# The attention-out projection and router norm of 24 row tiles in the last unit of the first attention

## The chip, the cores and the metric

One core of a Trainium2 chip runs the whole program. The metric is the device time in microseconds (us); the median of three runs is given, and one more execution was profiled. PE is TensorE (PEld its weight loads), DVE VectorE, ACT ScalarE, POOL GpSimd, SP SyncE.

## The reference

Four layers run one after the other on x of 4 x 1024 x 128, in float32, each on the layer norm of its input and added to it. The change touches the seam between the first two:

```
x = x + u + concat_heads(softmax(q k^T / sqrt(8)) v) @ w_out + b_out     # u = layernorm(x), 16 heads of 8; q, k, v from a second norm of u
z = layernorm(x)                                                     # (x - mean) * rsqrt(var + 1e-5)
logits = z @ Wr^T + rb                                               # 8 experts, the two best weighted by their sigmoid
x = x + shared(z) + sum over e of weight_e * expert_e(z)             # expert(z) = silu(z Wg^T) * (z Wu^T) @ Wd^T
```

After them come a differential attention and a feed-forward layer in blockwise FP4, which the change leaves as they are.

## The kernel before

The residual x lies in SBUF as 32 row tiles of 128 rows, which are 8 chunks of 4 tiles (two chunks to a batch element). The program is a row of blocks; each block gives every engine its own list of instructions, engines meet at a block's end, and within a block they are ordered by semaphores alone. There is no scheduler: the order in the code is the order on each engine.

**First attention** (`attention_phase`, from L419). It works in 16 units (a batch element and 4 heads of 8 channels). A unit has 16 steps k, eight for each half of the queries. In a step PE makes four score matmuls (L719; 51 rows of bf16 parts, 512 queries), ACT takes the exponential of each into `probs` (L656), and PE multiplies the probabilities of two steps earlier with v (L694). Scores go round three PSUM banks, so a score waits for the exponential three before it. The product with v stands after the second score of a step, in the steps k = 2 and 10 after the fourth. In these two steps ACT also copies a finished half of the output (L644, at the head of its step), PE transposes it back to rows (L702), and DVE divides it by the row sums into `o_units` (L601, L604). Beside this, PE and DVE compute the maxima of the next unit's scores (L676, L572). The last unit has no next one, so its banks 3 to 6 are nearly free, and DVE does little in it but round the FP4 weights (`fp4_round`, L622, with lines L2204 to L2250) in step k = 2. POOL is idle from the start of the attention, where it adds u and b_out to x.

**Weight transposes** (`transpose_jobs`, L946 to L964) are a block of their own.

**Router phase** (`attention_out_and_router_phase`, from L751), again a block. Each chunk goes through these stages, every engine taking several chunks at different stages in turn (`steps`, L776):
transposes of the attention output (PE L793), copy to SBUF (ACT L831), projection with w_out (PE L802, two passes to a matmul), addition to x (DVE L859), statistics (DVE L105, L109), 1/deviation and shift (POOL L116, L118, L883, L886), normalised rows z (ACT L840), transposes of z (PE L810), two copies of them, `zb` and the rounded `zH` (ACT L848, L849), the remainder `zL` (DVE L866), logits (PE L818) and their bias (DVE L871). A bank pair serves each of the four PSUM uses, so a chunk waits for the chunk two before it.

**Experts** (`experts_phase`, from L1102) begin with DVE's choice of experts, and SP loads the weights of the next attention.

Of the kernel before, what the change touches and what calls it, by code (L numbers as in the profile page):

```python
# [20 lines left out]
F32 = mybir.dt.float32  # L21
# [6 lines left out]
P = 128  # L28
# [118 lines left out]
class Stacks:  # L147
# [7 lines left out]
    def __init__(self, core, ctx, q_parts_dram, k_parts_dram):  # L155
# [6 lines left out]
        self.neg_rest, self.neg_parts = sb("neg_max_rest", [pairs, P]), sb("neg_max_parts", [pairs, PARTS, P], BF16)  # L162
        self.u, self.bo = sb("u", [P, core.tiles, core.C]), sb("b_out_rows", [P, core.C])
# [255 lines left out]
def attention_phase(core, v_units, o_units, stacks, fp4_weights, later):  # L419
# [55 lines left out]
    with ExitStack() as ctx:  # L475
# [20 lines left out]

        def units(engine, unit):


            for u in range(UNITS):  # L500
                unit(u, u // RING, u % RING, u % 2)
# [25 lines left out]
        with nc.Block() as block:  # L527
# [135 lines left out]
            def _(pe):  # L663
# [87 lines left out]
def attention_out_and_router_phase(core, o_units, w, zH, zL, logits, wrT, rb):  # L751
# [5 lines left out]
    nc, ps, C = core.nc, core.ps, core.C  # L757
    E = wrT.shape[1]
    TC = BANK // P
    CHUNKS = core.tiles // TC  # L760
    OT, OUT, ZT, LOGITS = 0, 2, 4, 6
    Z, TZ, LG = 2, 3, 4
    with ExitStack() as ctx:
        sb = lambda name, shape, dt=F32: sbuf(core.nc, ctx, name, shape, dt)
        oT, z, zb = sb("o_chunk_T", [P, 2, BANK]), sb("z_rows", [P, 2, TC, C]), sb("z_chunk_T", [P, 2, BANK])
        norm = Norm(core, ctx, "router", TC, CHUNKS)
        shift = sb("router_shift", [P, CHUNKS, TC])
        oT_psum, oT_ready = semaphore(core, "o_chunk_T_psum"), semaphore(core, "o_chunk_T_ready")
        out_psum, x_done = semaphore(core, "out_psum"), semaphore(core, "out_added")
        shifted, z_ready, zT_psum = semaphore(core, "router_shift_ready"), semaphore(core, "z_ready"), semaphore(core, "zT_psum")  # L770
        zb_ready, zH_done, zL_done = semaphore(core, "z_chunk_T_ready"), semaphore(core, "expert_zH_done"), semaphore(core, "expert_zL_done")
        lg_psum, lg_done = semaphore(core, "logits_psum"), semaphore(core, "logits_done")
        tile = lambda t: slice(t * P, (t + 1) * P)
        tiles = lambda c: slice(c * TC, (c + 1) * TC)

        def steps(*stages):  # L776

            for s in range(CHUNKS + LG):
                for lag, stage in stages:
                    if 0 <= s - lag < CHUNKS:  # L780
                        stage(s - lag)

        with nc.Block() as block:

            @block.tensor
            def _(pe):

                def transpose_o(c):
                    b, half = divmod(c, 2)
                    if c >= 2:  # L790
                        pe.wait_ge(oT_ready, c - 1)
                    for t in range(TC):
                        ins = nc.tensor.transpose(ps[:, OT + c % 2, tile(t)],  # L793
                                                  o_units[:, half * TC + t, b * GROUP:(b + 1) * GROUP, :].rearrange("p g c -> p (g c)"), core.ident[:])
                    ins.then_inc(oT_psum, 1)

                def project_o(c):
                    pe.wait_ge(oT_ready, c + 1)
                    if c >= 2:
                        pe.wait_ge(x_done, c - 1)  # L800
                    for t in range(TC):
                        ins = nc.tensor.matmul(ps[:, OUT + c % 2, tile(t)], oT[:, c % 2, tile(t)], w[:], start=True, stop=True)  # L802
                    ins.then_inc(out_psum, 1)

                def transpose_z(c):
                    pe.wait_ge(z_ready, c + 1)
                    if c >= 2:
                        pe.wait_ge(zL_done, c - 1)
                    for t in range(TC):
                        ins = nc.tensor.transpose(ps[:, ZT + c % 2, tile(t)], z[:, c % 2, t, :], core.ident[:])  # L810
                    ins.then_inc(zT_psum, 1)

                def make_logits(c):
                    pe.wait_ge(zb_ready, c + 1)
                    if c >= 2:
                        pe.wait_ge(lg_done, c - 1)
                    for t in range(TC):
                        ins = nc.tensor.matmul(ps[:, LOGITS + c % 2, t * E:(t + 1) * E], zb[:, c % 2, tile(t)], wrT[:],  # L818
                                               start=True, stop=True)
                    ins.then_inc(lg_psum, 1)  # L820

                steps((0, transpose_o), (TZ, transpose_z), (LG, make_logits), (0, project_o))

            @block.scalar
            def _(act):

                def copy_oT(c):
                    act.wait_ge(oT_psum, c + 1)
                    if c >= 2:
                        act.wait_ge(out_psum, c - 1)  # L830
                    nc.scalar.copy(oT[:, c % 2, :], ps[:, OT + c % 2, :]).then_inc(oT_ready, 1)  # L831

                def make_z(c):
                    act.wait_ge(norm.inverse, c + 1)
                    act.wait_ge(shifted, 2 * c + 2)
                    if c >= 2:
                        act.wait_ge(zT_psum, c - 1)
                    for t in range(TC):
                        n = c * TC + t
                        ins = nc.scalar.activation(z[:, c % 2, t, :], core.x[:, n, :], ACT.Identity,  # L840
                                                   bias=shift[:, c, t:t + 1], scale=norm.rstd[:, n:n + 1])
                    ins.then_inc(z_ready, 1)

                def take_zT(c):
                    act.wait_ge(zT_psum, c + 1)
                    if c >= 2:
# [1621 lines left out]
```

## Time and profile before

| | us |
|---|---|
| median of 3 runs | 2914.62 (2912.93 to 2914.83) |
| the profiled execution | 2917.84 |
| its span, first to last instruction | 2916.1 |
| PE busy in the span | 2753.1 (94%) |
| DVE busy | 2377.3 (82%) |
| ACT busy | 1997.7 (69%) |
| POOL busy | 1040.0 (36%) |
| mean granted TensorE clock | 0.975 of full |

The 3.2 us between the median and the profiled execution are to be kept in mind when stretches of the profile are subtracted from the median. A granted clock of 1.00 is 2.4 GHz and one of 0.50 is 1.2 GHz. Busy PE time contains the latency of matmuls, so a busy PE can still have room. The last unit of the attention runs from about 748 to 792 us, the weight transposes to 801, the router phase to 843.

### The profile page before, as it was taken

Reading aid. Unit: us, or ns where it says so; the run is one execution under the profiler, and the core shown is the slowest. Engines: PE = TensorE matmul, PEld = TensorE weight load, DVE = VectorE, ACT = ScalarE, POOL = GpSimd, SP = SyncE. Lnnn points to the kernel's source line nnn. Section 1 sums busy time; section 2 is a strip of 40 time slices with the busy share of each in tenths; the row PEclk is TensorE's granted clock in tenths of the full one; section 3 lists DMA queues with packets and bytes.
Section 4 is the critical chain, followed back from the end, with each engine's and each line's share of the span. In section 5 each row is a group of like instructions: output and inputs, shape, how many; then the busy total and the mean of one; then the engine's idle time right before and its main releaser. Section 6 shows DMA issues by size and latency. Waiting matters only on the chain.

```text
span 2916.1 us, 43834 instructions
## 1 busy us (share of the span) xinstructions
PE 2753.1 (94%) x14770; PEld 1820.7 (62%) x14770; DVE 2377.3 (82%) x3982; ACT 1997.7 (69%) x3999; POOL 1040.0 (36%) x1558
## 2 busy tenths in 40 slices
PE   4799999999889999899999999999999999999996
PEld 2122222222278888777777777777777777777774
DVE  6999999999355555677777888888888889888887
ACT  5288888888742232477777777777777777777773
POOL 4200000000010000145555665555555556555561
PEclk8699999999979999999999999999999999999998
DMA  2220000000010000000000000000000000000000
GB/s 66 87 80 19 17 23 23 17 18 13 1 59 1 1 1 1 1 1 1 1 1 1 1 1 1 1 1 1 8 1 1 1 1 8 1 1 1 1 1 15
DMA packets 31023, 34.98 MB, mean 12 GB/s; under 512 B 7656, under 2 KB 18896, under 8 KB 30672
## 3 DMA queue, kind: packets, MB, share of 16 engines
q1 hardware_dynamic: 30800, 32.18, 3.7%
q8 instruction: 119, 1.95, 0.3%
q14 instruction: 104, 0.85, 0.1%
HBM read 23.37 MB, written 8.39 MB: 11 GB/s over the span
## 4 chain that ended last, share of the span: by engine, by line
PE 49%; DVE 8%; issue 2%; ACT 0%; POOL 0%; POOLq 0%; DVEq 0%; ACTq 0%
PE ps L1613 7%; PE ps L1614 7%; PE ps L1618 7%; PE ps L1552 7%; PE ps L1540 7%; DVE neg_maxima L1821 3%; PE ps L1568 2%; PE ps L1570 1%; PE ps L1569 1%; PE ps L1558 1%; PE ps L1557 1%; PE ps L1556 1%; PE ps L1529 1%; PE ps L1530 1%; PE ps L1531 1%
## 5 line engine op out<-in xcount | busy, mean ns | idle before, releaser
L1821 DVE TENSOR_REDUCE neg_maxima<-ps 128x1 f32<-128x1024 f32 x512 | 624.7, 1220 | 147.9 <-PE ps L1618 144.9
L656 ACT ACTIVATE probs<-ps 128x512 f32<-128x512 f32 x1024 | 535.1, 606 | 172.4 <-PE ps L719 172.2
L1763 ACT ACTIVATE diff_probs<-ps,neg_maxima 128x1024 f32<-128x1024 f32 x512 | 575.6, 1124 | 92.4 <-DVE neg_maxima L1821 90.4
L572 DVE TENSOR_REDUCE maxima_of_halves<-ps 128x2 f32<-128x1024 f32 x512 | 602.4, 1220 | 17.3 <-PE ps L676 12.8
L1613 PE MATMUL ps<-z_T_high,y_high 128*128 128x512 f32 x1024 | 464.9, 454 | 5.6 <-ACT diff_probs L1763 5.6
L2095 POOL TENSOR_TENSOR DT_low<-DT_whole,DT_high 128x512 fp32r<-128x512 f32 x256 | 334.9, 1308 | 351.8 <-DVEq L1989 306.4
L1614 PE MATMUL ps<-z_T_low,y_high 128*128 128x512 f32 x1024 | 404.5, 395 | 0.0
L1833 DVE SCALAR_TENSOR_TENSOR D<-diff_probs,ratio 128x1024 f32<-128x1024 f32 x256 | 330.1, 1290 | 9.4 <-DVE ratio L1829 0.4
L719 PE MATMUL ps<-q_stacks,k_stacks 51*128 51x512 bf16 x1024 | 314.1, 386 | 20.6 <-ACT probs L656 14.7
L1618 PE MATMUL ps<-z_T_high,y_low 128*128 128x512 f32 x1024 | 319.5, 393 | 0.0
L1540 PE MATMUL ps<-identity,D 128*128 128x128 f32 x2048 | 307.6, 273 | 1.7 <-ACT arena L1705 1.7
L676 PE MATMUL ps<-k_stacks,q_stacks 48*128 48x512 bf16 x1024 | 253.8, 403 | 40.9 <-DVE maxima_of_halves L572 32.6
L1540 PEld LDWEIGHTS ps<-identity,D 128*128 128x128 f32 x2048 | 254.5, 140 | 51.5 <-ACT arena L1705 2.6
L694 PE MATMUL ps<-probs,v_and_one 128*32 128x512 f32 x2048 | 274.9, 609 | 0.2 <-ACT probs L656 0.2
L719 PEld LDWEIGHTS ps<-q_stacks,k_stacks 51*128 51x128 bf16 x1024 | 77.4, 94 | 316.3 <-ACT probs L656 282.7
L116 POOL TENSOR_SCALAR router_rstd<-router_moments 128x4 f32<-128x4 f32 x8 | 1.8, 228 | 730.4 <-DVE router_moments L109 730.4
L1202 ACT ACTIVATE silu_gate<-ps 128x512 f32<-128x512 f32 x144 | 85.9, 597 | 246.8 <-PE ps L1173 246.8
L1720 ACT ACTIVATE squares<-ps,inverse_sums 128x256 f32<-128x256 f32 x256 | 122.4, 478 | 158.7 <-PE ps L1570 151.7
L1552 PE MATMUL ps<-arena,z_tiles 128*128 128x512 f32 x512 | 230.5, 593 | 0.0
L1613 PEld LDWEIGHTS ps<-z_T_high,y_high 128*128 128x128 f32 x1024 | 193.6, 189 | 54.8 <-issue 16.1
L1614 PEld LDWEIGHTS ps<-z_T_low,y_high 128*128 128x128 f32 x1024 | 194.2, 190 | 46.1 <-issue 15.1
L1618 PEld LDWEIGHTS ps<-z_T_high,y_low 128*128 128x128 f32 x1024 | 193.1, 189 | 45.2
(301 smaller groups left out, 5009.8 us busy)
## 6 DMA issues: line engine op xcount, KB each, us to landing
q_stacks<-q_parts_dram SPq DMA_DIRECT2D x192, 32.0 KB
q_parts_dram<-qk_parts SPq DMA_DIRECT2D x12, 256.0 KB, 2.4
k_parts_dram<-qk_parts SPq DMA_DIRECT2D x12, 256.0 KB, 3.4
k_stacks<-k_parts_dram SPq DMA_DIRECT2D x32, 96.0 KB
residual<-in_L_attn_x_dram SPq DMA_DIRECT2D x4, 512.0 KB, 6.2
k_stacks<-k_parts_dram SPq DMA_DIRECT2D x32, 64.0 KB
q_stacks<-neg_max_parts SPq DMA_DIRECT2D x96, 4.0 KB, 1.7
out_dram<-residual SPq DMA_DIRECT2D x3, 512.0 KB, 3.2
```

The source lines that it names most:

```text
L572: nc.vector.tensor_reduce(mx_half[:, own, half, :, p * PB + t, :], ps[:, bank:bank + 2, :], X, ALU.max).then_inc(nat_max, 1)
L656: nc.scalar.activation(probs[:, k % PT, h, :], ps[:, (r + k + i) % S_RING, :], ACT.Exp, scale=SCALE).then_inc(s_free, 1)
L719: nc.tensor.matmul(ps[:, (r + k + i) % S_RING, :], kst[rows, r, p, kb * P:(kb + 1) * P], qst[rows, r, p, half * BANK:(half + 1) * BANK], s ...
L1540: ins = nc.tensor.transpose(ps[:, T_BANK, k * P:(k + 1) * P], D[:, t % 2, kb * P:(kb + 1) * P], core.ident[:])
L1552: nc.tensor.matmul(ps[:, UY, :], z[:, k, :], DT[:, g, k, :], start=k == 0, stop=False)
L1613: nc.tensor.matmul(ps[:, 2 * m + c, :], a, high[:, keys], start=True, stop=False)
L1614: nc.tensor.matmul(ps[:, 2 * m + c, :], a, low[:, keys], start=False, stop=False)
L1618: ins = nc.tensor.matmul(ps[:, 2 * m + c, :], a_low, high[:, keys], start=False, stop=True)
L1763: nc.scalar.activation(probs[:, t % 2, m, :], ps[:, 2 * m:2 * m + 2, :].rearrange("p k n -> p (k n)"), ACT.Exp, bias=neg[:, t, m:m + 1], a ...
L1821: nc.vector.tensor_reduce(neg[:, t, m:m + 1], ps[:, 2 * m:2 * m + 2, :].rearrange("p k n -> p (k n)"), X, ALU.max, negate=True).then_inc(m ...
L1833: nc.vector.scalar_tensor_tensor(D[:, t % 2, :], probs[:, t % 2, 1, :], ratio[:, t:t + 1], probs[:, t % 2, 0, :], ALU.mult, ALU.add).then_ ...
L2095: pool.tensor_tensor(DT_low[:, t // G, :, q], DT_whole, DT_high[:, t // G, :, q].bitcast(F32), ALU.subtract).then_inc(DT_split, 1)
```

## The change

- Chunks 0 to 5 (24 row tiles) are transposed (even steps 0 to 10) and projected (odd steps 1 to 11) inside the last attention unit, at the end of the step on PE, in banks 4 and 6. DVE, not ACT, copies the transposes to SBUF there, then adds to x and takes the statistics. `fp4_round` comes after the last of these chunks.
- POOL computes 1/deviation of these chunks in the same block, and the normalised rows of chunks 0 to 3. Rows of chunks 4 and 6 are ACT's, of 5 and 7 DVE's.
- The router phase projects only chunks 6 and 7 and does the rest of the stages for all eight. The order on each engine is written out.
- z rows get six slots, in the place of `u`. `gate` and `h` of the experts are allocated earlier.

```diff
@@ attention_phase: GpSimd
                 pool.tensor_tensor(core.x[:], core.x[:], stacks.bo[:].rearrange("p (o c) -> p o c", o=1).to_broadcast(
-                    [P, core.tiles, core.C]), ALU.add)
+                    [P, core.tiles, core.C]), ALU.add).then_inc(u_added, 1)
+                pool.wait_ge(u_added, 2)
+                for c in range(router.FRONT):
+                    router.deviation(pool, c)
+                    if c < router.POOL_ROWS:
+                        router.pool_rows(pool, c)
@@ attention_phase: VectorE
-                        if k == LAG and not exists(u + 1):
-                            dve.wait_ge(fp4_weights.arrived, 16 * len(fp4_weights.loads))
-                            fp4_round(dve, fp4_rounder, stepper(dve, fp4_rounded), fp4_weights.w[:], fp4_weights.w[:])
                         if k == PB + LAG:
                             divide_o(u, 0, *turn_of(u, odd, ("o", 0)))
+                        if k in chunk_out and not exists(u + 1):
+                            c = chunk_out[k]
+                            if c == 0:
+                                dve.wait_ge(u_added, 2)
+                            router.wait_oT(dve, c)
+                            nc.vector.tensor_copy(router.oT[:, c % 2, :], ps[:, CHUNK_OT, :]).then_inc(router.oT_ready, 1)
+                            router.add(dve, c, CHUNK_OUT)
+                            if c == router.FRONT - 1:
+                                dve.wait_ge(fp4_weights.arrived, 16 * len(fp4_weights.loads))
+                                fp4_round(dve, fp4_rounder, stepper(dve, fp4_rounded), fp4_weights.w[:], fp4_weights.w[:])
@@ attention_phase: TensorE, at the end of a step
+                        if k in chunk_T and not exists(u + 1):
+                            if k == 0:
+                                pe.wait_ge(nat_max, last_turn + 1 + NAT0)
+                                pe.wait_ge(expert_weights.arrived, 16 * len(expert_weights.loads))
+                            router.transpose_o(pe, chunk_T[k], o_units, CHUNK_OT, chunk_T[k] > 0)
+                        if k in chunk_out and not exists(u + 1):
+                            router.project_o(pe, chunk_out[k], expert_weights.w_out, CHUNK_OUT, chunk_out[k] > 0)
@@ class Router (the stages of the old function, with these new or different)
+    SLOTS = 6
+    FRONT = 6
+    POOL_ROWS = 4
+    ACT_ROWS, DVE_ROWS = (4, 6), (5, 7)
...
+    def deviation(self, pool, c):
+        norm, shift = self.norm, self.shift[:, c, :]
+        norm_rstd(norm, pool, c, c)
+        if c in self.ACT_ROWS:
+            use = 2 * self.ACT_ROWS.index(c)
+            pool.wait_ge(norm.inverse, c + 1)
+            pool.tensor_tensor(shift, norm.moments[:, self.tiles(c), 0], norm.rstd[:, self.tiles(c)], ALU.mult).then_inc(self.shifted, 1)
+            pool.wait_ge(self.shifted, use + 1)
+            pool.tensor_scalar(shift, shift, -1.0, None, ALU.mult).then_inc(self.shifted, 1)
+
+    def pool_rows(self, pool, c):
+        pool.wait_ge(self.norm.inverse, c + 1)
+        for t in range(self.TC):
+            ins = norm_rows(self.norm, pool, self.z[:, c, t, :], self.core.x[:, c * self.TC + t, :], c * self.TC + t)
+        ins.then_inc(self.z_pool, 1)
@@ router_phase
+                for c in last:
+                    router.transpose_o(pe, c, o_units, OT + c % 2, False)
+                router.transpose_z(pe, 0)
+                router.transpose_z(pe, 1)
+                for c in last:
+                    router.project_o(pe, c, w, OUT + c % 2, False)
+                for c in range(router.CHUNKS):
+                    router.make_logits(pe, c, zb, wrT)
+                    if c + 2 < router.CHUNKS:
+                        router.transpose_z(pe, c + 2)
...
+                for c in last:
+                    router.wait_oT(act, c)
+                    act.copy(router.oT[:, c % 2, :], core.ps[:, OT + c % 2, :]).then_inc(router.oT_ready, 1)
+                for c in range(router.CHUNKS):
+                    if c == 2:
+                        router.scalar_rows(act, 4)
+                    if c == 5:
+                        router.scalar_rows(act, 6)
+                    router.take_zT(act, c, zb, zH)
...
+                router.vector_rows(dve, 5)
+                for n, c in enumerate(last):
+                    router.add(dve, c, OUT + c % 2)
+                    router.low_z(dve, n, zH, zL)
+                router.take_logits(dve, 0, logits, rb)
+                for c in range(2, router.CHUNKS):
+                    if c == 3:
+                        router.vector_rows(dve, 7)
+                    router.low_z(dve, c, zH, zL)
+                    router.take_logits(dve, c - 1, logits, rb)
+                router.take_logits(dve, router.CHUNKS - 1, logits, rb)
...
+                for c in last:
+                    router.deviation(pool, c)
```

A norm row (`norm_rows`) is one tensor_scalar with two per-row operands, 128x128 in and out, on the engine that it is given.

## Rows read from the trace of the kernel before

**Rows 1.** Windows: us and instructions busy per engine, granted clock, DMA.
```profile
750.00:790.00 40.00, 32.61 (x198) 7.65 (x194) 10.31 (x14) 31.42 (x62) 0.00 (x0) 0.96 0.00 0
...
800.00:844.80 44.80, 35.29 (x195) 32.82 (x196) 23.85 (x104) 25.16 (x58) 13.66 (x32) 0.67 0.00 1
```

**Rows 2.** Timeline of one step of the last unit: start, duration, instruction.
```profile
762.68 2.06 ACT L656 ACTIVATE probs<-ps 128x512 f32<-128x512 f32 x4 [0.33 <-PE ps L719]
...
763.33 0.39 PE L719 MATMUL ps<-q_stacks,k_stacks 51*128 51x512 bf16 x1 [0.47 <-ACT probs L656]
763.65 1.06 PE L694 MATMUL ps<-probs,v_and_one 128*32 128x512 f32 x8
...
764.64 0.60 PE L719 MATMUL ps<-q_stacks,k_stacks 51*128 51x512 bf16 x3
765.07 2.06 ACT L656 ACTIVATE probs<-ps 128x512 f32<-128x512 f32 x4 [0.33 <-PE ps L719]
```

**Rows 3.** Timeline of the router phase, PE.
```profile
801.47 1.09 PE L793 MATMUL ps<-identity,arena 128*128 128x128 f32 x4 [1.69 <-PEq L934]
...
806.83 2.08 PE L802 MATMUL ps<-w_out,o_chunk_T 128*128 128x128 f32 x8 [0.68 <-ACT o_chunk_T L831]
...
815.93 0.60 PE L810 MATMUL ps<-identity,z_rows 128*128 128x128 f32 x4
...
816.36 0.96 PE L818 MATMUL ps<-wrT,z_chunk_T 128*128 128x8 f32 x8
...
817.18 1.14 PE L802 MATMUL ps<-w_out,o_chunk_T 128*128 128x128 f32 x8
...
818.15 0.60 PE L793 MATMUL ps<-identity,arena 128*128 128x128 f32 x4
```

**Rows 4.** Timeline of the last unit where ACT copies the output, k = 10.
```profile
773.21 0.59 ACT L644 COPY oT<-ps 128x512 f32<-128x512 f32 x1
...
776.74 1.08 ACT L656 ACTIVATE probs<-ps 128x512 f32<-128x512 f32 x2 [0.97 <-PE ps L719]
```

**Rows 5.** Windows and timeline where the granted clock is at its lower level.
```profile
754.00:756.00 2.00, 2.00 (x10) 0.82 (x6) 0.37 (x2) 0.14 (x1) 0.00 (x0) 0.50 0.00 0
...
810.00:814.00 4.00, 3.56 (x16) 3.38 (x16) 2.34 (x13) 2.52 (x7) 1.72 (x4) 0.50 0.00 0
...
756.19 1.08 ACT L656 ACTIVATE probs<-ps 128x512 f32<-128x512 f32 x2 [2.05 <-PE ps L719]
```

**Rows 6.** Timeline of the router phase, DVE and ACT.
```profile
805.34 0.69 DVE L859 TENSOR_TENSOR residual<-ps,residual 128x512 f32<-128x512 f32 x1 [4.20 <-PE ps L802]
...
807.11 0.38 DVE L109 BATCH_NORM_AGGREGATE router_moments<-router_stats 128x2 f32<-128x6 f32 x4
...
815.44 0.56 ACT L848 COPY z_chunk_T<-ps 128x512 f32<-128x512 f32 x1
...
816.52 0.69 DVE L866 TENSOR_TENSOR z_T_low<-ps,z_T_high 128x512 fp32r<-128x512 f32 x1 [1.53 <-ACT z_T_high L849]
...
817.18 1.65 ACT L840 ACTIVATE z_rows<-residual,router_shift,router_rstd 128x128 f32<-128x128 f32 x4 [0.21 <-issue]
```

**Rows 7.** Timeline, the end of the router phase.
```profile
842.85 0.19 DVE L871 TENSOR_TENSOR logits<-ps,rb_rows 128x32 f32<-128x32 f32 x1 [1.32 <-PE ps L818]
```

**Rows 8.** Timeline of DVE in the last unit: the FP4 rounding, the last divide.
```profile
756.10 1.34 DVE L2204 TENSOR_REDUCE fp_weights_scale<-fp_w 128x72 f32<-128x1152 f32 x1
...
764.35 1.36 DVE L2250 TENSOR_TENSOR fp_w<-fp_weights_scaled,fp_weights_scale 128x1152 f32<-128x1152 f32 x1
...
791.23 0.26 DVE L601 RECIPROCAL recip<-ps 128x16 f32<-128x16 f32 x1 [14.21 <-PE ps L702]
```

**Rows 9.** Groups by line, POOL: busy us, mean ns, idle before.
```profile
L2095 POOL TENSOR_TENSOR DT_low<-DT_whole,DT_high 128x512 fp32r<-128x512 f32 x256 | 334.9, 1308 | 351.8 <-DVEq L1989 306.4 <-ACT DT_high L1705 41.2 <-DVEq L2029 2.5
...
L118 POOL TENSOR_TENSOR router_rstd<-router_rstd,minus_half 128x4 f32<-128x4 f32 x8 | 8.3, 1036 | 0.7 <-POOL router_rstd L116 0.2
...
L1304 POOL CAST M_head<-M 128x256 fp32r<-128x256 f32 x32 | 12.5, 392 | 34.0 <-ACT M L1374 34.0
```

More of the change, by code:

```diff
@@ L495, in attention_phase @@
         S0, NAT0, PV0 = S_RING, NAT_BUFS, PT
+        CHUNK_OT, CHUNK_OUT = NAT + 1, NAT + 3
+        chunk_T = {2 * c: c for c in range(router.FRONT)}
+        chunk_out = {2 * c + 1: c for c in range(router.FRONT)}
+        last_turn = taken[UNITS - 2, ("shift", 0)]
         def units(engine, unit):
@@ L748, in _ @@
                 transpose_o(UNITS - 1, 1, *turn_of(UNITS, 0, ("o", 1)))
-def attention_out_and_router_phase(core, o_units, w, zH, zL, logits, wrT, rb):
-    nc, ps, C = core.nc, core.ps, core.C
-    E = wrT.shape[1]
+class Router:
     TC = BANK // P
-    CHUNKS = core.tiles // TC
-    OT, OUT, ZT, LOGITS = 0, 2, 4, 6
-    Z, TZ, LG = 2, 3, 4
-    with ExitStack() as ctx:
[L764 to L783, printed above, removed]
@@ new lines, in transpose_o, with project_o @@
+    def transpose_o(self, pe, c, o_units, bank, reused):
+        b, half = divmod(c, 2)
+        if reused:
+            pe.wait_ge(self.oT_ready, c)
+        for t in range(self.TC):
+            ins = pe.transpose(self.core.ps[:, bank, self.tile(t)],
+                               o_units[:, half * self.TC + t, b * GROUP:(b + 1) * GROUP, :].rearrange("p g c -> p (g c)"), self.core.ident[:])
+        ins.then_inc(self.oT_psum, 1)
+    def project_o(self, pe, c, w, bank, reused):
+        pe.wait_ge(self.oT_ready, c + 1)
+        if reused:
+            pe.wait_ge(self.x_done, c)
+        for t in range(self.TC):
+            ins = pe.matmul(self.core.ps[:, bank, self.tile(t)], self.oT[:, c % 2, self.tile(t)], w[:], start=True, stop=True)
+        ins.then_inc(self.out_psum, 1)
@@ new lines, in make_logits, with wait_oT @@
+    def make_logits(self, pe, c, zb, wrT):
+        E = wrT.shape[1]
+        pe.wait_ge(self.zb_ready, c + 1)
+        if c >= 2:
+            pe.wait_ge(self.lg_done, c - 1)
+        for t in range(self.TC):
+            ins = pe.matmul(self.core.ps[:, self.LOGITS + c % 2, t * E:(t + 1) * E], zb[:, c % 2, self.tile(t)], wrT[:],
+                            start=True, stop=True)
+        ins.then_inc(self.lg_psum, 1)
+    def wait_oT(self, engine, c):
+        engine.wait_ge(self.oT_psum, c + 1)
+        if c >= 2:
+            engine.wait_ge(self.out_psum, c - 1)
@@ new lines, in wait_slot, with scalar_rows @@
+    def wait_slot(self, engine, c):
+        engine.wait_ge(self.norm.inverse, c + 1)
+        if c >= self.SLOTS:
+            engine.wait_ge(self.zT_psum, c - self.SLOTS + 1)
+    def scalar_rows(self, act, c):
+        self.wait_slot(act, c)
+        act.wait_ge(self.shifted, 2 * self.ACT_ROWS.index(c) + 2)
+        for t in range(self.TC):
+            n = c * self.TC + t
+            ins = act.activation(self.z[:, c % self.SLOTS, t, :], self.core.x[:, n, :], ACT.Identity,
+                                 bias=self.shift[:, c, t:t + 1], scale=self.norm.rstd[:, n:n + 1])
+        ins.then_inc(self.z_act, 1)
@@ new lines, in pool_rows, with router_phase @@
+    def pool_rows(self, pool, c):
+        pool.wait_ge(self.norm.inverse, c + 1)
+        for t in range(self.TC):
+            ins = norm_rows(self.norm, pool, self.z[:, c, t, :], self.core.x[:, c * self.TC + t, :], c * self.TC + t)
+        ins.then_inc(self.z_pool, 1)
+def router_phase(core, router, o_units, w, zH, zL, logits, wrT, rb):
+    OT, OUT = 0, 2
+    with ExitStack() as ctx:
+        zb = sbuf(core.nc, ctx, "z_chunk_T", [P, 2, BANK])
+        last = range(router.FRONT, router.CHUNKS)
+        with core.nc.Block() as block:
@@ L797, in project_o @@
[L797 to L811, printed above, removed]
@@ L2431, in program @@
         fp4 = Fp4Transposed(core, ctx, fp4_weights)
+        router = Router(core)
+        with ExitStack() as ahead_of_rows:
+            router.place_norm(ahead_of_rows)
         rows = DifferentialRows(core, ctx)
```

146 lines of the change are left out of this document (72 added, 74 removed).

## The prediction

> **What bounds the kernel now.** I read the busy times by stretch first [rows 1]. In the last attention unit (750 to 790 us) PE is busy for 32.6 of 40 us and ACT for 31.4; nothing is saturated there. In the router phase (800 to 844.8) PE shows 35.3 of 44.8 us at a mean granted clock of 0.67, while DVE and ACT are busy for a little over half and POOL for 13.7: a chain that hands chunks from engine to engine, with TensorE often at its lower level. All engines meet at the end of each block, so a microsecond taken out of either stretch is a microsecond of the span, provided that nothing behind waits for it.
>
> Second, one regular step of the last unit in order of time [rows 2]. The exp at 762.68 frees a bank; the score matmul at 763.33 takes it (0.65 us later), the products with v start at 763.65 (0.32), the next scores at 764.64 (0.99), and their exp at 765.07 (0.43): 2.39 us. In this loop ACT works 2.06 and stands 0.33, and PE waits 0.47 before the score at 763.33. So there is a hole in PE, but the loop through PE and ACT is closed: what is put on PE is free only as far as it fits in the hole.
>
> Third, the pieces of the router phase [rows 3 to 6], and where it ends: the last logits at 842.85 + 0.19 = 843.04 [rows 7].
>
> **The change part by part.**
>
> *What the last unit takes on.* Per chunk of four row tiles PE gets four transposes T (in even steps 0 to 10) and four projections P (odd steps 1 to 11), all behind the step's last score. Prices at the full clock: T 0.43 us (815.93 to 816.36), P 0.97 (817.18 to 818.15); at the half clock T shows 1.09 and P 2.08, the latency of the last instruction with them [rows 3], so I take 0.87 and 1.8 from start to start.
> A P starts about 0.2 us before the loop's reference exp (its two scores start 0.43 ahead of that exp and take some 0.2 to 0.3), so it ends 0.8 after it. The next scores start there, not at once; the second of them was due at 0.65. The products with v then start at about 0.8 + 0.32 = 1.12 to 1.25 in place of 0.97: 0.15 to 0.3 us later, and I take 0.3 for steps 3, 5, 7 and 11 = 1.2. In steps 1 and 9 ACT copies oT next in any case (0.59 us in front of the exps) [rows 4], which covers a P: 0.05 each. A T ends 0.3 after the reference exp, before anything is due: 0.05 each for steps 0, 4, 6, 8. In steps 2 and 10 the unit's own transposes already let ACT run dry (0.97 us idle before the exp at 776.74 [rows 4]); a second T there costs itself, 0.5 with the change-over, twice = 1.0. Sum 1.2 + 0.1 + 0.2 + 1.0 = **+2.5 us**. Bounds: below, 0 (no piece can make the unit faster, except that a busier PE might spare the half-clock stretch of [rows 5], worth at most 1.1 us: the stall of 2.05 there against 0.97 in the same place of the other half); above, every piece in full, 6 x (0.97 + 0.43) = 8.4.
>
> *DVE in the last unit.* Copy, addition and statistics per chunk: 0.69 + 2.15 (805.34 to 807.49) [rows 6] = 2.8 us in 4.8 us of two steps. The copy has a whole step between T and P, so no wait enters PE. fp4_round (756.10 to 765.71, 9.6 us) [rows 8] moves from step 2 behind the last chunk. The last P starts near 778.0 in old time, ends at 779.0, its addition and statistics at 781.3, the rounding at 790.9; the last divide, which is queued behind it, was released at 791.23 [rows 8]. So the margin is 0.3 us, more by what the last P delays the rest. I put 0 for it; if DVE is late by a microsecond, that is on the path, for the block's end waits for this divide.
>
> *POOL.* Deviations of six chunks and rows of four. A deviation costs 1.04 for the power [rows 9], and I allow 0.8 for its small instructions. A row instruction (128x128, one tensor in) stands nowhere; from below a cast of 128x256 takes 0.39, from above a 128x512 with two tensors 1.31 [rows 9]; I take 0.5, for it is nearer to the cast. A chunk is then 1.8 + 4 x 0.5 = 3.8 us, at the upper bound 7.0; six chunks beginning at 753 end by 782, or by 785 at the upper bound, and the first reader (transpose of z chunk 0) stands at 803. Hidden at either end.
>
> *What the router phase gives.* Chunks 6 and 7 alone are still projected there; eight are transposed, split and given logits. It begins as before at 801.47 [rows 3], TensorE at the half clock until about 814 [rows 5]. PE's order: T6, T7, z0, z1, four pieces of 0.87: 804.9. P6, P7 at 1.8: 808.5. Logits 0 (a P's price, eight passes): 810.3. z2 wants the low part of chunk 0, which DVE makes behind addition and statistics of chunk 6: 807.0 + 2.15 + 0.69 = 809.9, in time. z2 811.2, logits 1 813.0, z3 813.9, logits 2 about 815.0. From here, at the full clock, PE needs 0.97 + 0.43 = 1.4 us a chunk and is no longer the bound; z4 ends 815.5, logits 3 816.5. DVE makes rows 7 in four instructions (1.3 us; below 0.69 by the price of 512 elements in the addition, above 1.65, ACT's [rows 6]) at 813.7 to 815.1, so low 3 ends at 815.8 and z5 at 817. ACT takes z4 (zb 0.56 [rows 6], and zH as long, overlapping: 1.0 together) until 816.7 and only then makes rows 6 (1.65), until 818.4: z6 waits for it and ends at 818.9. ACT's copies of chunk 5 end at 819.4, of 6 at 820.4; low 5 at 820.2, z7 820.7, zb 7 at 821.4, logits 7 822.6, the addition of rb 823.0. Against 843.04: **-20.0 us**. Bounds by the clock, with the same order: half speed to the end, 2.7 us a chunk on PE, ends at 828.9 (-14.1); full speed from the start, bound by DVE and ACT, ends at 818.9 (-24.1).
>
> *What stands behind.* SP's loads of the next attention's weights start at the next block and shift with it; its first waits are on instructions, not on clock time. gate and h only get other addresses. The PE wait for expert weights in step 0 is long met. All 0.
>
> Sum: 2.5 - 20.0 = -17.5. The profiled execution took 2917.84 us (span 2916.1); it would become 2900.3. The median of the three timed runs is 2914.62, 3.2 below the profiled one, and the forecast for the median is 2914.62 - 17.5 = **2897.1**.
>
> **The rivals.**
> - *The half clock holds through the router phase.* For it: it holds from 801 to 814 and returns several times later, mean 0.67 [rows 1, 5]. Against: PE will be idle less than before. -14.1 + 2.5 = -11.6: 2903.0.
> - *The full clock comes early*, since attention's end keeps PE busier: 2.5 - 24.1 = -21.6: 2893.0. For it, the same sentence; against, the start of this phase stays what it is, a block's end with PE idle 1.7 us [rows 3].
> - *The pieces cost their full price in the last unit*, because the loop of [rows 2] has less play than I drew: 8.4 - 20.0 = -11.6: 2903.0 too. For it: ACT is only 0.33 from being full. Against: PE's wait of 0.47 in each step.
> - *Slower: the last unit falls to the half clock.* Its place is the 38 us of the unit; the profile shows one such stretch in it, 754 to 757 [rows 5]. There the loop of [rows 2] would take 3.75 (the products with v doubled, the scores' latency up by a half), with a T or P in PE 4.3 on the mean, against 2.39 and 2.6: 12 x 1.7 + 4 x 1.4 = +26. Net -17.5 + 26 = +8.5: 2923. It makes the kernel slower only where over two thirds of the unit run so. Against it: 0.96 mean clock in the unit with less work on PE than it will have [rows 1].
> - *DVE late.* The rounding has 0.3 us to spare, and POOL's last deviation (1.8 us) runs beside its start. If DVE stood still for that time, the last divide would come 1.5 late: -16.0, 2898.6; with as much again in the last chunk's statistics, -14.2, 2900.4. For it: four of the rounding's ten instructions read two SBUF tensors. Against: POOL's power takes 1.04 us [rows 9] in the router phase while DVE works too [rows 6], with no sign of either being held up. The Trainium skill (GPSIMD Engine Reference, Key points) has the rule for it: GpSimd shares its SBUF interfaces with VectorE, and contends with DVE instructions that have two SBUF inputs or run in a 2-port mode. The rows cited have no such DVE instruction beside POOL, so they don't decide on that rule.
>
> **How the numbers follow.** Forecast 0.45; half clock 0.14, early full clock 0.17, full price 0.13, DVE late 0.07, slower 0.03; 0.01 for a gain undone elsewhere. 0.2% is 5.8 us, about what can be told from no change here. All but the last two lie beyond it unless half clock and full price meet (-5.7). So faster 0.92, same 0.05, slower 0.03. The range reaches from the early clock with a free unit (-23) to half clock with two thirds of the full price (-8): 2892 to 2907.
>
> **What would show it.** The last unit (first scores of unit 15 to the last divide) should be 2 to 4 us longer, its steps 3, 5, 7 and 11 at 2.6 to 2.7 us and its plain even ones at 2.4. The first weight transpose should follow the last divide by 0.6 us as before, and the divide should wait for PE. POOL's rows should last 0.4 to 0.8 each. The router phase should be 21 to 23 us from its first transpose to the last logits, half clock until about 814. From the expert phase on every stretch should keep its length. The forecast is wrong if steps with a P take over 3 us, if DVE's rounding ends after the last transposes, or if z transposes wait for rows.

## The result and the profile after

The changed kernel takes 2896.2 us (median of four runs, 2894.97 to 2896.72) against 2913.77 of the kernel before (four runs): 17.6 us less, ratio 0.9939 (0.9922 to 0.9956). The forecast was 2897.1. The profiled execution took 2894.97 us, its span is 2893.1.

I cut both profiles by instructions that exist in both: VectorE's copy of v for the last unit, the last divide, the last logits, the first and the last maximum of the second attention. Instructions by line in the kernel before: durations in ns (min/median/max), then the first and the last start in us.

```profile
L608 DVE COPY v_and_one<-arena x16: 271/284/285, 119.3 to 740.5; 128x256 f32<-128x256 f32 x16
L601 DVE RECIPROCAL recip<-ps x32: 257/257/258, 148.3 to 791.2; 128x16 f32<-128x16 f32 x32
L1821 DVE TENSOR_REDUCE neg_maxima<-ps x512: 1210/1219/1226, 1210.9 to 2842.8; 128x1 f32<-128x1024 f32 x171
```
The same in the changed kernel, and its logits:
```profile
L622 DVE COPY v_and_one<-arena x16: 273/283/284, 118.0 to 738.6; 128x256 f32<-128x256 f32 x16
L615 DVE RECIPROCAL recip<-ps x32: 257/258/259, 146.4 to 790.1; 128x16 f32<-128x16 f32 x32
L911 DVE TENSOR_TENSOR logits<-ps,rb_rows x8: 179/180/193, 808.4 to 822.4; 128x32 f32<-128x32 f32 x8
L1920 DVE TENSOR_REDUCE neg_maxima<-ps x512: 1209/1219/1227, 1189.6 to 2819.1; 128x1 f32<-128x1024 f32 x171
```

| stretch | before | after | difference |
|---|---|---|---|
| start to the v copy of the last unit | 740.5 | 738.6 | -1.9 |
| v copy to the last divide ("the unit") | 50.7 | 51.5 | +0.8 |
| last divide to the last logits ("the phase") | 51.6 | 32.4 | -19.3 |
| last logits to the first maximum | 368.1 | 367.2 | -0.9 |
| first to last maximum of the second attention | 1631.9 | 1629.5 | -2.4 |
| the rest of the span | 73.3 | 74.0 | +0.7 |

Differences are taken from hundredths (the last divide is at 791.23 and 790.06, the last logits at 842.85 [rows 7] and 822.42). "The phase" contains the weight transposes, which take the same time in both; the router phase itself, from its first transposes to the last logits, went from 41.4 us (801.47 to 842.85) to 22.1 (800.30 to 822.42).

The change made the second and third rows, -18.5 together. The rest of the profiles' difference of 22.9 is of the size of the scatter of single executions: it lies in stretches with the same instructions, and the v copy of the other kernels' profiles below lies between 738.6 and 740.9.

The last unit after, timeline, steps with a P (L833) and a T (L824) between two full exp rows of ScalarE:
```profile
757.60 2.06 ACT L677 ACTIVATE probs<-ps 128x512 f32<-128x512 f32 x4 [0.17 <-PE ps L740]
...
759.57 0.39 PE L740 MATMUL ps<-q_stacks,k_stacks 51*128 51x512 bf16 x2
759.89 1.16 PE L833 MATMUL ps<-w_out,o_chunk_T 128*128 128x128 f32 x8
759.99 1.08 ACT L677 ACTIVATE probs<-ps 128x512 f32<-128x512 f32 x2 [0.33 <-PE ps L740]
...
760.98 0.39 PE L740 MATMUL ps<-q_stacks,k_stacks 51*128 51x512 bf16 x2
...
761.46 1.08 ACT L677 ACTIVATE probs<-ps 128x512 f32<-128x512 f32 x2 [0.38 <-PE ps L740]
...
762.62 0.66 PE L824 MATMUL ps<-identity,arena 128*128 128x128 f32 x4
762.72 2.06 ACT L677 ACTIVATE probs<-ps 128x512 f32<-128x512 f32 x4 [0.17 <-PE ps L740]
```
Two steps take 5.12 us (757.60 to 762.72) where two of before take 4.78 (twice the 2.39 of [rows 2]): 0.34 us for a P and a T together, which add 1.40 us of work to PE.

The half clock near step 2 of the kernel before cost more than the one stall of [rows 5]. ScalarE before, in steps 2 and 3 and in the same place of the other half, steps 10 and 11:
```profile
752.04 2.10 ACT L656 ACTIVATE probs<-ps 128x512 f32<-128x512 f32 x4
...
757.90 2.06 ACT L656 ACTIVATE probs<-ps 128x512 f32<-128x512 f32 x4 [0.62 <-PE ps L719]
...
773.67 2.10 ACT L656 ACTIVATE probs<-ps 128x512 f32<-128x512 f32 x4
...
778.00 2.06 ACT L656 ACTIVATE probs<-ps 128x512 f32<-128x512 f32 x4 [0.17 <-PE ps L719]
```
From the first to the second are 5.86 us, from the third to the fourth 4.33: the stretch at half clock cost 1.5 us. In the changed kernel it is gone.

The router phase after: windows with the granted clock, as in [rows 1, 5], then PE's steady state.
```profile
803.00:806.00 3.00, 1.82 (x18) 1.73 (x16) 2.62 (x11) 2.52 (x7) 0.43 (x2) 1.00 0.00 0
806.00:810.00 4.00, 2.75 (x21) 2.72 (x21) 3.62 (x15) 1.69 (x4) 2.53 (x5) 0.89 0.00 0
810.00:814.00 4.00, 4.00 (x21) 4.00 (x21) 2.09 (x7) 2.61 (x7) 0.00 (x0) 0.50 0.00 0
```
```profile
810.71 1.09 PE L846 MATMUL ps<-identity,z_rows 128*128 128x128 f32 x4
...
811.60 1.72 PE L855 MATMUL ps<-wrT,z_chunk_T 128*128 128x8 f32 x8
...
813.17 1.09 PE L846 MATMUL ps<-identity,z_rows 128*128 128x128 f32 x4
```
The clock is full until 809.1 us and half from there past the end of the phase, the reverse of what I had drawn; a chunk then takes 2.46 us (810.71 to 813.17).

### The profile page after: what moved, and what is told of

Its sections match the earlier page's. It is cut to its first block, busy times and chain, and to the rows that moved or that the text cites. A ratio compares the mean times of both kernels' runs of the same rounds, so it can differ in the third digit from the quotient of the medians.

```text
span 2893.1 us, 43818 instructions
## 1 busy us (share of the span) xinstructions
PE 2739.3 (95%) x14770; PEld 1815.6 (63%) x14770; DVE 2382.3 (82%) x3996; ACT 1985.1 (69%) x3969; POOL 1049.1 (36%) x1562
## 4 chain that ended last, share of the span: by engine, by line
PE 49%; DVE 7%; issue 2%; ACT 0%; POOL 0%; POOLq 0%; DVEq 0%; ACTq 0%
PE ps L1712 7%; PE ps L1713 7%; PE ps L1717 7%; PE ps L1651 7%; PE ps L1639 7%; DVE neg_maxima L1920 3%; PE ps L1667 2%; PE ps L1669 1%; PE ps L1668 1%; PE ps L1657 1%; PE ps L1656 1%; PE ps L1655 1%; PE ps L1628 1%; PE ps L1629 1%; PE ps L1630 1%
## 5 line engine op out<-in xcount | busy, mean ns | idle before, releaser
L586 DVE TENSOR_REDUCE maxima_of_halves<-ps 128x2 f32<-128x1024 f32 x512 | 602.3, 1220 | 16.8 <-PE ps L697 12.4
```

Source lines behind the costliest of these rows:

```text
L586: nc.vector.tensor_reduce(mx_half[:, own, half, :, p * PB + t, :], ps[:, bank:bank + 2, :], X, ALU.max).then_inc(nat_max, 1)
```

## The experiments

"Unit" and "phase" are the stretches of the table, from each run's profile. "Half clock" is the first stretch at half clock behind the last unit: where it begins, in us behind the last divide, and how long it lasts (from windows of half a microsecond; the router phase itself begins 10.2 behind the divide, in low_first and front7b_fill 11.1). Medians are of 4 to 10 runs beside the kernel before on the same chip (2911.7 to 2914.4).

| kernel | unit | phase | half clock | median |
|---|---|---|---|---|
| before | 50.7 | 51.6 | 10.1, for 13.7 | 2913.8 |
| changed | 51.5 | 32.4 | 19.1, for 17.1 | 2896.2 |
| after_again | 51.5 | 32.8 | 16.2, for 20.5 | 2896.0 |
| rows_by_act | 51.5 | 34.9 | 19.7, for 20.5 | 2898.8 |
| pool_rows_alone | 50.7 | 53.5 | 10.1, for 13.7 | 2915.7 |
| double_P | 56.9 | 34.2 | 10.1, for 3.4 | 2902.8 |
| no_pieces | 50.8 | 32.8 | 16.7, for 20.5 | 2896.5 |
| low_first | 51.5 | 32.8 | 1.7, for 3.4 | 2897.1 |
| filler2 | 51.5 | 31.7 | 10.4, for 3.4 | 2896.8 |
| front7 | 56.8 | 31.1 | 10.7, for 3.4 | 2898.4 |
| front7b | 52.6 | 28.4 | 17.9, for 17.1 | 2896.6 |
| filler_all | 51.5 | 36.0 | 20.2, for 20.5 | 2894.8 |
| front7b_fill | 52.6 | 26.8 | 1.4, for 3.4 | 2892.8 |
| front7b_fill_again | 52.6 | 25.9 | 34.9, behind the phase | 2891.4 |

**after_again**, the changed kernel once more.

> The changed kernel as it is. Theory (PE's added work keeps the clock up): the granted clock stays at full level through the last attention unit and is still full when the router phase begins, and the first transposes of that phase take half of what they took before (0.5 to 0.6 us for four, not 1.09); time 2895 to 2898. Rival (where the clock falls is chance): the first stretch of the router phase is at half clock in this run, and the phase is 2 to 6 us longer than the 22.3 us of the first profile.

The lengths repeat to half a microsecond, full clock at the start of the phase included, but the clock falls 2.9 us earlier in the phase. That the full clock at the start belongs to the change is not shown: filler2 below has it otherwise.

**rows_by_act**, the part that GpSimd does, undone.

> GpSimd makes no rows; ScalarE makes those of chunks 0 to 3 too, in the router phase, 4 x 1.65 us, the first two ahead of its first copy. Theory (the gain is mostly the six chunks' chain of transposes, projection, addition and statistics that left the phase; ScalarE had 6.9 us of waits for TensorE in it): 2 to 4 us slower than the changed kernel, 2898 to 2900. Rival (GpSimd's rows carry a large part of the gain): the full 6.6 us are lost, 2903.

```diff
-    POOL_ROWS = 4
-    ACT_ROWS, DVE_ROWS = (4, 6), (5, 7)
+    POOL_ROWS = 0
+    ACT_ROWS, DVE_ROWS = (0, 1, 2, 3, 4, 6), (5, 7)
@@ ScalarE, router phase
+                router.scalar_rows(act, 0)
+                router.scalar_rows(act, 1)      # ahead of the copies of oT; 2 and 3 ahead of take_zT 0 and 1
```

Phase +2.2 to 2.6, time +2.6 to 2.8 us, and no run of either kernel lies among the other's: the theory. So some 2.5 of the 17.6 us are due to rows on GpSimd, the rest to the move together with the new order of the stages and the six slots, which no run takes apart (front7b comes nearest).

**pool_rows_alone**, the same part alone in the kernel before.

> The kernel before with one part of the change alone: GpSimd makes the rows of chunks 0 to 3 in the router phase, in the old order of stages. Theory: it costs time, since four rows take GpSimd 3.1 us where ScalarE took 1.65, and with 1.7 us of deviation GpSimd needs 4.8 us a chunk against a period of 3.4 to 4.3: 2 to 5 us slower than before, 2916 to 2919. Rival (taking 1.65 us a chunk off ScalarE is a gain by itself): 3 to 6 us faster, 2908 to 2911.

```diff
 def make_z(c):                                  # ScalarE
+    if c < 4:
+        return
@@ GpSimd, behind the deviation of chunk c
+                    if c < 4:
+                        for t in range(TC):
+                            ins = norm_rows(norm, pool, z[:, c % 2, t, :], core.x[:, c * TC + t, :], c * TC + t)
+                        ins.then_inc(z_pool, 1)
```

2915.68 against 2912.07: slower by 3.6 us in the medians, as the theory has it (2 to 5), but the ratio is 1.0009 (1.0 to 1.0019), whose interval reaches down to no change. The rival's gain of 3 to 6 us is excluded. Timeline of GpSimd:
```profile
807.52 3.15 POOL L128 TENSOR_SCALAR z_rows<-residual,router_moments,router_rstd 128x128 f32<-128x128 f32 x4
810.64 0.24 POOL L116 TENSOR_SCALAR router_rstd<-router_moments 128x4 f32<-128x4 f32 x1
...
812.09 3.13 POOL L128 TENSOR_SCALAR z_rows<-residual,router_moments,router_rstd 128x128 f32<-128x128 f32 x4
```
GpSimd has no idle time here and makes a chunk in 4.57 us (807.52 to 812.09), more than the old period of 3.4 to 4.3. The same rows that save 2.5 us when they are made in advance save nothing in the chain, where the phase of the profile is 1.9 us longer.

**double_P**, what a microsecond more on PE costs in the unit.

> The changed kernel with every projection of the last unit issued twice (same result), 0.97 us more of TensorE work in six steps. Theory (the loop of scores, exp and products with v closes over TensorE, and the hole is filled by the first projection): each costs its full price, 0.9 to 1.0 x 6 = 5.5 us: 2901 to 2902.5. Rival (ScalarE bounds the unit and TensorE's work is hidden): the second costs what the first did, 0.34 in four steps: 2897.5.

```diff
-        for t in range(self.TC):
+        for t in (tuple(range(self.TC)) * 2 if twice else range(self.TC)):
             ins = pe.matmul(self.core.ps[:, bank, self.tile(t)], self.oT[:, c % 2, self.tile(t)], w[:], start=True, stop=True)
```

Unit +5.4. Its exp rows in steps that answer to those shown above:
```profile
760.03 2.06 ACT L677 ACTIVATE probs<-ps 128x512 f32<-128x512 f32 x4 [0.17 <-PE ps L740]
762.42 1.09 ACT L677 ACTIVATE probs<-ps 128x512 f32<-128x512 f32 x2 [0.33 <-PE ps L740]
764.78 1.08 ACT L677 ACTIVATE probs<-ps 128x512 f32<-128x512 f32 x2 [1.28 <-PE ps L740]
766.04 2.07 ACT L677 ACTIVATE probs<-ps 128x512 f32<-128x512 f32 x4 [0.17 <-PE ps L740]
```
Two steps now take 6.01 us, 0.89 more for 0.97 more of PE work, and ScalarE waits 1.28 where it waited 0.38. The first projection costs 0.34, a second one nearly its full price: the hole in PE's step is real and the first piece fills it. The median is 6.6 us above the changed kernel's; the unit explains 5.4 of it, and the phase is 1.4 to 1.9 us longer in this profile, which is of the slowest of the five runs and has half clock at the start of the router phase.

**no_pieces**, what the pieces cost and do to the clock.

> The changed kernel without the twelve pieces on TensorE in the last unit: transposes and projections of chunks 0 to 5 are left out (VectorE copies and adds x itself in their place, with the same waits), so the result is another. Theory (TensorE's load decides the clock, and a piece costs 0.34 us at the steps with a projection and 0.4 at the two with output transposes): the unit's plain steps all take 2.39 us, the stretch at half clock near step 2 comes back (1.1 us), and the router phase begins at half clock as in the kernel before; time 2894 to 2898, no better than with the pieces. Rival (the clock does not depend on them): the unit is 2 us shorter, the router phase unchanged: 2894.

```diff
@@ TensorE (VectorE adds a copy of x in the place of the projection)
-                            router.transpose_o(pe, chunk_T[k], o_units, CHUNK_OT, chunk_T[k] > 0)
+                            pe.sem_inc(router.oT_psum, 1)
...
-                            router.project_o(pe, chunk_out[k], expert_weights.w_out, CHUNK_OUT, chunk_out[k] > 0)
+                            pe.wait_ge(router.oT_ready, chunk_out[k] + 1)
+                            pe.sem_inc(router.out_psum, 1)
```

The unit is 0.7 us shorter than with the pieces, as long as before, and the half clock near step 2 is back. Windows of no_pieces, then of the changed kernel:
```profile
754.00:756.00 2.00, 2.00 (x12) 0.71 (x4) 0.00 (x0) 0.53 (x2) 1.92 (x3) 0.50 0.00 0
...
800.00:806.00 6.00, 4.31 (x40) 4.25 (x39) 3.83 (x12) 3.84 (x10) 0.00 (x0) 1.00 0.00 0
```
```profile
754.00:756.00 2.00, 2.00 (x20) 1.16 (x12) 0.03 (x1) 1.79 (x4) 2.00 (x4) 1.00 0.00 0
```
The half-clock stretch near step 2 stands in all three profiles without the pieces (before, pool_rows_alone, no_pieces) and in none of the eleven with them. It costs 1.5 us here too (ScalarE's two steps take 5.85 and 4.32 us), so the pieces themselves cost 0.7 + 1.5 = 2.2 us. The second half of my theory fell: the phase begins at full clock without them as well.

Nor does the start at half clock belong to the kernel before alone. In filler2, whose instructions up to the logits of chunk 0 are those of the changed kernel, the clock fell 0.2 us into the first transposes. The eight of the changed kernel, those of filler2, and a window of filler2:
```profile
800.30 1.06 PE L824 MATMUL ps<-identity,arena 128*128 128x128 f32 x8 [1.69 <-PEq L1033]
```
```profile
801.35 1.76 PE L824 MATMUL ps<-identity,arena 128*128 128x128 f32 x8 [1.69 <-PEq L1041]
```
```profile
802.00:804.00 2.00, 2.00 (x12) 2.00 (x11) 0.47 (x2) 1.17 (x2) 0.00 (x0) 0.50 0.04 8
```
Five of the fourteen profiles fall between 10.1 and 10.7 us behind the last divide, where PE has just been idle for 1.69 us or starts again: before, pool_rows_alone, double_P, filler2 and front7. What sets the two old ones apart is the length, 13.7 us against 3.4. There PE idles again before each P (0.68 [rows 3]), where now sixteen transposes and two projections follow without a gap; that this keeps the clock down is likely, not shown. Why the clock falls at this place in some executions and not in others stays open.

**low_first**, VectorE's order.

> The changed kernel with another order on VectorE in the router phase: the low part of z chunk 0 before the addition of chunk 6, that of chunk 1 before the addition of chunk 7. Theory (TensorE's two waits of 1.2 us each before the transposes of z chunks 2 and 3 are for the low parts, queued behind statistics): both waits shrink below 0.5 us and the phase is 1 to 2.4 us shorter: 2894 to 2895. Rival (after 809 us TensorE at half clock is the bound and the statistics of 6 and 7 come later): nothing gained, 2896.

```diff
+                router.low_z(dve, 0, zH, zL)
+                router.add(dve, 6, OUT)
+                router.low_z(dve, 1, zH, zL)
+                router.add(dve, 7, OUT + 1)
-                for n, c in enumerate(last):
-                    router.add(dve, c, OUT + c % 2)
-                    router.low_z(dve, n, zH, zL)
```

Nothing gained in the median. The wait moved: z2's is gone and z3's down from 1.21 to 0.42, but logits 2 now wait for VectorE's addition of logits 0, behind the statistics of chunk 7. The router phase itself takes 21.8 us against 22.1 and 22.5; 0.8 us of this profile's phase was lost in the weight transposes before it, at half clock. Timeline of low_first:
```profile
807.84 0.63 PE L846 MATMUL ps<-identity,z_rows 128*128 128x128 f32 x4 [0.42 <-DVE z_T_low L905]
...
809.97 1.85 PE L855 MATMUL ps<-wrT,z_chunk_T 128*128 128x8 f32 x8 [1.50 <-DVE logits L911]
```

**filler2**, four idle transposes of the identity after the logits of chunks 0 and 1.

> The changed kernel with four idle 128x128 transposes of the identity (0.97 us at full clock) after the logits of chunks 0 and 1, in the place of TensorE's two waits. Theory (the clock falls at 809 because TensorE waited from 804.8 to 808.7): the fall comes later or not at all in the router phase, which ends 2 to 4 us earlier: 2892 to 2894. Rival (the fall comes from earlier idle time or is unmoved): same or up to 0.5 us slower, 2896 to 2896.5.

The phase is 0.6 us shorter, the time 0.6 longer: no effect that these runs can tell. The clock did stay full from 805 to 815 us, but it had been at half for 3.4 us before, so this profile doesn't decide on the theory.

**front7**, a seventh chunk in the unit.

> The changed kernel with a seventh chunk in the last unit (transposes at step 12, projection at step 13), the FP4 rounding spread over VectorE's gaps between chunks, and VectorE's low parts of z 0 and 1 ahead of the one addition left. Theory: 0.34 us more in the unit; the router phase loses one set of transposes, a projection and an addition with statistics (2.2 us on VectorE before the low part of chunk 1): 2 to 4 us shorter, so 2892 to 2894.5. Rival (behind 809 us TensorE's 2.45 us a chunk decides whatever comes before): under 1 us, 2895 to 2896.

```diff
-    FRONT = 6
+    FRONT = 7
...
@@ VectorE, last unit, behind the addition of chunk c (in place of fp4_round behind the last one)
+                            for part in {1: (0, 1), 2: (2, 3), 3: (4,), 5: (5, 6, 7), 6: (8, 9)}.get(c, ()):
+                                fp4_part(dve, fp4_rounder, fp4_step, fp4_weights.w[:], part)
@@ VectorE, router phase
+                router.low_z(dve, 0, zH, zL)
+                router.add(dve, 7, OUT + 1)
+                router.low_z(dve, 1, zH, zL)
```

The phase is 1.3 us shorter, but the unit 5.3 longer. Timeline of front7 at step 13:
```profile
785.44 1.16 PE L837 MATMUL ps<-w_out,o_chunk_T 128*128 128x128 f32 x8 [1.77 <-DVE o_chunk_T L642]
...
786.85 1.87 PE L717 MATMUL ps<-probs,v_and_one 128*32 128x512 f32 x8
```
Three parts of the rounding (2.9 us) stood before the copy of chunk 6, the projection waited 1.77 for it, and the products with v behind it took 1.87 in place of 1.07: the clock had fallen.

**front7b**, the same with shorter parts in that place.

> As front7, with the rounding's parts moved so that no copy of a chunk waits behind them (one part of 0.76 us each after chunks 4 and 5, the last three after chunk 6). Theory (front7 lost 5.3 us in the last unit only because the projection of chunk 6 waited 1.8 us for VectorE and the clock then fell for 6.8 us): the unit takes 51.8 to 52 us from its v copy to its last divide, the router phase keeps the 1.5 us that front7 gained: 2894 to 2895. Rival (a seventh chunk doesn't fit in the unit): the unit stays over 54 us, 2897 or more.

```diff
-{1: (0, 1), 2: (2, 3), 3: (4,), 5: (5, 6, 7), 6: (8, 9)}
+{1: (0, 1), 2: (2, 3), 3: (4,), 4: (5,), 5: (6,), 6: (7, 8, 9)}
```

The unit is 52.6 (half a microsecond above the theory, far below the rival), the phase 28.4, together 2.9 us less than in the changed kernel; yet the median is 2896.6. The profiled execution, 2895.3, was the fastest of the four. Where the others lost it stays open. The router phase itself takes 18.2 us here and 21.8 in low_first, which has the same order on VectorE and whose clock fell at the same place in it (7.6 and 7.7 us behind its start): 3.6 us less for one more chunk moved. That is the nearest thing here to the price of the move alone.

**filler_all** and **front7b_fill**, two idle transposes after the logits of every chunk, in the changed kernel and in front7b.

> The changed kernel with two idle 128x128 transposes of the identity (0.5 us at full clock) after the logits of every chunk in the router phase. Theory (at 2.45 us a chunk TensorE at half clock bounds the phase from 809 us on, although its records show no gap, and 8-column logit matmuls are light work that leaves it there): with more columns the clock returns within the phase, a chunk then takes 1.9 us, and the phase is 1 to 3 us shorter, 2893 to 2895. Rival (the clock is not raised by this): half clock to the end with 1 us more a chunk, up to 6 us slower: 2899 to 2902.

> front7b and the two idle transposes after the logits of each chunk together. Theory: if both help alone, their gains add: 2891 to 2893. Rival (clock not raised): 2898 to 2900.

```diff
                     router.make_logits(pe, c, zb, wrT)
+                    for _ in range(2):
+                        pe.matmul(core.ps[:, OUT, 0:P], core.ident[:], core.ident[:], start=True, stop=True)
```

filler_all scattered from 2892.3 to 2901.7. Its profile is of the slowest run, and shows the rival: half clock from 812 us, phase 36.0. front7b_fill has the clock full through the router phase, which takes 15.6 us; it was at half for 3.4 us in the weight transposes before it. Windows of filler_all, then of front7b_fill, and PE's steady state there:
```profile
815.00:820.00 5.00, 5.00 (x25) 5.00 (x25) 1.49 (x4) 2.50 (x6) 0.00 (x0) 0.50 0.00 2
```
```profile
810.00:815.00 5.00, 5.00 (x48) 5.00 (x47) 3.12 (x10) 3.90 (x9) 0.52 (x1) 1.00 0.00 0
815.00:820.00 5.00, 5.00 (x47) 4.96 (x45) 2.56 (x7) 2.88 (x6) 0.00 (x0) 1.00 0.02 5
```
```profile
813.75 0.96 PE L859 MATMUL ps<-wrT,z_chunk_T 128*128 128x8 f32 x8
814.57 0.69 PE L960 MATMUL ps<-identity 128*128 128x128 f32 x4
815.09 0.60 PE L850 MATMUL ps<-identity,z_rows 128*128 128x128 f32 x4
815.53 0.96 PE L859 MATMUL ps<-wrT,z_chunk_T 128*128 128x8 f32 x8
```
A chunk takes 1.78 us (813.75 to 815.53) with the idle work in it, against 2.46 without it at half clock.

**front7b_fill_again.**

> The same kernel again, with more rounds. If the gain over the changed kernel (2896) is real, the median is 2891 to 2894; in the profile the router phase (last divide to last logits) takes 26 to 27 us at full clock, or 29 to 33 where the clock falls in it. Rival (the first four times were luck of where the clock falls): 2895 to 2898.

2891.44 (2890.32 to 2893.45), ratio to the kernel before 0.9925 (0.9911 to 0.9938); phase 25.9, the router phase itself 15.6 us as in the first series, full clock until 827. Both medians lie 3 to 5 us below the changed kernel's 2896, and the slowest of these nine runs (2893.45) is below the fastest of its eight (2894.97), though the chips differ and the intervals of the ratios to the kernel before overlap. This version very likely beats both kernels.

## Why the prediction was right, and where its steps were off

- *The last unit, +2.5.* Measured +0.8. The regular P cost 0.3 as said (0.34 with its T). The second T in step 10 cost 0.40 (ScalarE's gap from 773.67 to 776.74 before, from 771.70 to 775.17 after: 3.07 and 3.47), said 0.5. What I had only as a lower bound came true: the half-clock stretch of [rows 5] went, and step 2 took 3.48 in place of 4.15 us although it has a second T. So the term was mis-sized by 1.7, about 1.5 of it the clock: the pieces cost 2.2 to 2.3 us, close to the 2.5, and the stretch at half clock gave 1.5 back. The "at most 1.1" of my bound counted its one stall alone and left out the 0.45 us that step 3 lost (ScalarE's 1.71 us from 756.19 to 757.90 against 1.26 from 776.74 to 778.00).
- *DVE in the unit, 0.* Right: the rounding ended at 789.18 and the divide was released by PE at 790.06, so 0.9 us was left.
- *POOL, 0.* Right, with a wrong price: a row takes 0.79 us, not 0.5, and lay between my bounds of 0.39 and 1.31. Rows ended at 773.1.
- *The router phase, -20.0.* Measured -19.3 from divide to logits (-18.9 in the second profile). The size is right, the course was not. I had half clock to 814 and full clock behind; the chip gave full clock to 809 and half behind. The first six pieces took 3.6 us where I had 7.0, and z3 ended 9.0 us behind the start of the router phase, not 12.4; then a chunk took 2.46 us to the end, where I had 1.5 to 1.9 bound by VectorE and ScalarE. I was 3.4 us too slow before z3 and 4.1 too fast behind it: the two errors nearly cancelled, and that is luck. The low part of chunk 0 "in time" was wrong as well. PE, at full clock, was there first and waited 1.22 us for it, and 1.21 for that of chunk 1, both queued behind statistics. The wait of z6 for ScalarE's rows did not come, since PE was the slower.
- *Behind the phase, 0.* Right within the scatter: 368.1 and 367.2 us to the second attention.
- *The sum.* -17.5 forecast, -18.5 in the two stretches of the profiles, -17.6 in the medians: closer than the terms deserve.
- *The signs.* The router phase took 22.1 us (21 to 23 said), steps with a P 2.73 at most (over 3 would have been against it), the rounding ended before the last transposes, and no transpose waited for rows. The unit was not 2 to 4 us longer, and half clock did not come first.
- *The rivals.* None came true whole. "Half clock through the phase" and "full clock early" each held for a part of it, and the reason given for the second (a busier PE at attention's end) fell with no_pieces. "DVE late" was seen only in front7, which put more work there; where GpSimd and VectorE met, it was GpSimd that took longer (below). "Full price in the unit" was excluded by double_P: only the second P pays it.

## What to carry to other kernels

Work fits beside a pipelined loop in the gap of the engine that carries it, and only once: the first 1.4 us in two steps cost 0.34, the next 0.97 cost 0.89. A helper engine slower than the one it relieves pays when it works ahead of need, and saved nothing where it stood in the chain. When a short phase is re-timed, compute it at both clock levels for each part of it, take its profile more than once, and test an order on the chip: a wait taken away from one instruction came back at the next.

## What the runs showed of the hardware that I had not expected

- GpSimd and VectorE do get in each other's way, and in the pairs shown GpSimd is the one that waits. Timelines of front7b, GpSimd, then VectorE:
```profile
764.78 0.23 POOL L116 TENSOR_SCALAR router_rstd<-router_moments 128x4 f32<-128x4 f32 x1 [0.66 <-DVE router_moments L109]
...
769.90 1.18 POOL L116 TENSOR_SCALAR router_rstd<-router_moments 128x4 f32<-128x4 f32 x1 [0.53 <-DVE router_moments L109]
...
787.84 2.11 POOL L118 TENSOR_TENSOR router_rstd<-router_rstd,minus_half 128x4 f32<-128x4 f32 x1
```
```profile
769.66 1.32 DVE L2317 TENSOR_TENSOR fp_weights_scaled<-fp_w,fp_weights_inverse 128x1152 f32<-128x1152 f32 x1
...
787.71 1.36 DVE L2367 TENSOR_TENSOR fp_weights_scaled<-fp_weights_scaled,fp_weights_magic 128x1152 f32<-128x1152 f32 x1
```
The same GpSimd instruction takes 1.18 in place of 0.23 us when it starts beside a VectorE instruction with two SBUF inputs; it ends at 771.08, just behind that one's end at 770.98, which took no longer than in the kernel before (1.36 [rows 8] for an instruction of the kind). The power takes 2.11 in place of 1.04 [rows 9] beside two more of them, and the first instruction 0.57 beside one with a single SBUF input (781.23 to 781.96). In all of these VectorE's instruction had started first; the other order was not tried. The Trainium skill (GPSIMD Engine Reference, Key points) states this contention, and this trace agrees; the direction of the loss is from the trace. In the changed kernel itself no such pair shows: all sixteen rows take 0.79 to 0.81.
- PE records without a gap don't mean a working PE at full clock: in the steady state at half clock PE is busy for 4.00 of 4.00 us, and with 0.5 us more work per chunk a chunk was 0.68 us shorter at the higher level. That the idle transposes hold the clock up is the likely reading of front7b_fill against front7b (router phase at full clock in two profiles of two, at half from its middle in one of one), but filler_all, with the same idle work and waits of 0.68 and 0.67 us before z2 and z3, fell to half clock in its profile.
